# Bias products with a full contraction, a new order of the work between groups, and the second group's magnitude behind the first group's flags

## The chip, the cores and the metric

The kernel runs on 1 core of one Trainium2 chip. The metric is the device time in microseconds (us); lower is better. The engines are named as in the profile: PE is TensorE, DVE is VectorE, ACT is ScalarE, POOL is GpSimd, SP issues the transfers.

## The reference

A small transformer-like tower over 4 sequences of 512 tokens with 64 channels:

- token stage: for each sequence `weighted = where(mask, rel_dist, 0)`, `nbr = weighted @ neighbor_embed[ids] * w_rd`, then `h = [atom_embed[ids], nbr] @ w1 + b1`, a layer norm with gamma and beta, silu, `@ w2 + b2`.
- attention stage on the normalised h: `content`, `values` and `key_ph` are three projections of x with biases; `hop` and `ksk` are two-layer gelu networks that give query phases `tanh(...) * pi`, a width per head, and storage phases; cos and sin of these are features; the result is a causal (cumulative) sum over the sequence, which the kernel computes as scores against a triangle plus a running state, chunk by chunk. The five window weights `exp(-0.5 d^2 / width^2)` are folded into one phase (an arctangent of two sums) and one magnitude per head. A layer norm and an output projection follow.
- expert stage: 8 experts with 128 hidden units, the best two scores of each token chosen (`top 2`), `gelu(x @ W1 + b1) @ W2 + b2` summed over the chosen ones, with residuals to the output (4, 512, 64).

## The kernel before, in words

Four sequences make two groups (g = 0, 1) of two sequences each, side by side on the partitions. Each group has 8 tiles of 128 tokens (4 chunks times 2 sequences). For each group there are five stages, written as generators for each engine: `token` (T), `project` (P), `queries` (Q), `chunks` (C), `experts` (X), and `weights` (W) once. A generator gives up its turn at each `yield`. The list `ORDER` says in which order the pieces are issued, the same list on every engine: the third "P1" is the third piece of group 1's `project`. An engine runs its queue strictly in that order, and semaphores tie the engines to each other. So a piece that is moved in `ORDER` is moved past all that stands between, on every engine. In this text P1.3 means the third piece of P1.

The pieces that matter here:

- P1.1 (group 1): PE waits for the first query centres of group 0, runs ten filler products (`spin_products(n, bank)`, L624: n products of 128x512 bf16 into a bank that nobody reads), waits for x of group 1 and transposes it (L728). ACT copies the transposes to `x_t` (L447).
- P1.2: PE runs the position product (L761), then four "joint" products, one per chunk: a bias product (L735, stationary operand `ones[0:1, 0:P]`, one row, start of the accumulation) and the product with x_t (L737). Before, the order is joint 0, joint 1, `hop_and_gate` (L742, L745), joints 2 and 3. ACT copies each joint to `vk` (L453); joints 2 and 3 wait for the copies of 0 and 1, since they share two banks.
- P1.3: PE runs `storage` (L750, L752) and then fillers, each bunch behind a semaphore of group 0's query phases. ACT runs the gelus (L458 to L468).
- Q0.1 to Q0.8 and Q1.1 to Q1.8: window weights. Q.1: DVE L1303 to L1307, ACT exp (L489). Q.2: DVE phase base (L1314), ACT magnitude of the key phases (L495, Abs). Q.3: DVE window sums (L1320 to L1329), ACT key features by sine (L501). Q.4: DVE inverse root, the argument of the arctangent (L1340), then the query magnitude `mag` (L1342 to L1344); ACT, for group 1, eight multiplications of the stored keys (L509), then the arctangent (L512). Q.5: DVE phi and the phase sums (L1352 to L1362), ACT rounding (L518). Q.6: DVE L1368, ACT absolute value, sine, cosine. Q.7: DVE times `mag` (L1376). Q.8: DVE sums (L1383, L1387).
- C.1: PE transposes the key features into banks 4 and 5 (L843), ACT copies them (L542). C.2: the same for the queries (L860, L547). C.3: scores of chunk 0 (L871, L876). C.4 to C.7: per chunk the scores of the next one, the state product (L883, L885) and the outputs (L902 to L909); DVE masks the scores (L1401) and adds up the state (L1409, L1412). C.7: ACT squares and copies (L558, L559). C.8: PE variance and output projection (L927, L933), DVE inverse root (L1428 and behind). C.9: DVE `h3` (L1443), ACT its square.
- X.1: PE transposes h3 (L954). X.2: expert scores on PE (L963), the normalised x2 on DVE (L1466). X.3: low part of x2 on DVE (L1475), transposes on PE (L975), copies `xp1` on ACT (L583). X.4: DVE finds the two best experts and writes the flags (L1479 to L1497); PE, for group 0 only, runs 33 fillers behind semaphores. X.5: transposes with the flags (L995), copies `xp2` (L588). X.6 to X.24: n = 0 to 18, hidden products `hidden(n)` (L1014 with the high part of the weights, L1015 with the low part and the flags), gelu on ACT (L608), and second-layer products `back` (L1026, L1030). X.25: the results are turned back and added (L1041, L1049, L1507).

The group 0 experts (X0.6 on) run woven with the group 1 chunks (C1.2 on) in time on PE; after them the group 1 experts run alone.

Of the kernel before, what the change touches and what calls it, by code (L numbers as in the profile page):

```python
# [82 lines left out]
ORDER = ("T0 T0 T0 T0 T1 T1 T0 T0 T1 T0 T1 P0 P0 T1 P0 T1 Q0 P0 T1 W0 P0 Q0 P1 Q0 P1 Q0 C0 Q0 Q0 P1 Q0 Q0 P1 C0 "  # L83
         "C0 P1 C0 P1 C0 Q1 C0 Q1 C0 Q1 C0 C0 X0 X0 Q1 X0 C1 Q1 Q1 X0 Q1 X0 X0 X0 X0 Q1 X0 C1 C1 X0 C1 X0 C1 "
# [21 lines left out]
def tower(nc, ids, dist, mask, early, folded, late, ffn, mrows, out):  # L106
# [4 lines left out]
    with ExitStack() as ctx:  # L111
# [156 lines left out]
        hid_bank = (0, 1, 3)  # L268
        ksk_bank = (2, 6)
# [28 lines left out]
        def pair(t, c):  # L298
            return t[:, c, :, :].rearrange("p f d -> p (f d)")

# [103 lines left out]
        def _(act):  # L404
# [82 lines left out]
            def queries(g):  # L487
# [3 lines left out]
                act.wait_ge(S["kq_tanh"], g + 1)  # L491
                act.wait_ge(S["st_tanh"], g + 1)
                if g:
                    act.wait_ge(S["k_feat"], 2 * g)
                nc.scalar.activation(kph_abs[:], kph[:, g], ACT.Abs).then_inc(S["kph_abs_set"], 1)  # L495
                yield

                act.wait_ge(S["kph_abs_set"], g + 1)
# [6 lines left out]
                if g:  # L505
                    act.wait_ge(S["k_feat"], 2 * g + 1)
                    act.wait_ge(S["gcr_set"], 2)
                    for t in range(8):
                        ins = nc.scalar.mul(feat[:, g, 0, t, D:P], feat[:, g, 0, t, D:P], gcr[:, g, t:t + 1])  # L509
                    ins.then_inc(S["stored_q"], 1)  # L510
                act.wait_ge(S["at_arg"], g + 1)
                nc.scalar.activation(wscr[:, 3], wscr[:, 2], ACT.Arctan).then_inc(S["at_set"], 1)  # L512
# [60 lines left out]
            def experts(g):  # L573
# [7 lines left out]
                for k in range(2):  # L581
                    act.wait_ge(S["xp1_mm"], 2 * g + k + 1)
                    nc.scalar.copy(xp1[g][:, 512 * k:512 * k + 512], bank[x_bank[g] + k][:, :]).then_inc(S["xp1_set"], 1)  # L583
                yield
                yield
# [14 lines left out]
                for n in range(19):  # L600
                    if n == 10:
                        copy_y(0)
                    if n < 16:
# [4 lines left out]
                        nc.scalar.activation(hid[:, at % HB], bank[hid_bank[at % 3]][:, :], ACT.Gelu).then_inc(S["hid_set"], 1)  # L608
# [10 lines left out]
        def _(pe):  # L619
# [98 lines left out]
            def project(g):  # L718
                pe.wait_ge(late_in, 16)
                if g:  # L720
                    pe.wait_ge(S["center_set"], 1)
                    spin_products(10, 2)
# [10 lines left out]
                def joint(c, i):  # L733
                    if g:
                        nc.tensor.matmul(bank[i][:, 0:VK], ones[0:1, 0:P], K["vk_b"][0:1, :], start=True, stop=False)  # L735
# [30 lines left out]
                if g:  # L766
                    hop_and_gate()
                    last_joints()
                    yield
                    pe.wait_ge(S["h1_norm"], NG)  # L770
# [12 lines left out]
                    spin_products(4, 7)  # L783
# [46 lines left out]
            def chunks(g):  # L830
# [33 lines left out]
                def scores(c):  # L864
                    at = g * NC + c
                    pe.wait_ge(S["qtr_set"], 2 * g + c // 2 + 1)
                    pe.wait_ge(S["ktr_set"], 2 * g + 2)
                    if c:
# [74 lines left out]
            def experts(g):  # L943
# [33 lines left out]
                yield  # L977
                if g == 0:
# [634 lines left out]
```

## Time and profile before

| | |
|---|---|
| time, median of 3 runs | 165.93 us (165.22 to 165.97) |
| the profiled execution's own time | 166.21 us |
| its span, first to last instruction | 164.5 us (so 1.71 us lie around it) |
| PE busy | 151.8 us, 92% of the span, fillers included (L624: 120 recorded, 30.0 us) |
| DVE busy | 113.7 us, 69% |
| ACT busy | 83.6 us, 51% |
| mean granted TensorE clock | 0.976 of full speed |

PE looks full, but 30.0 us of it are fillers. Where fillers stand, PE is the bound only if they run past the event that the next real product waits for. So the share of busy time does not answer the question; in each stretch one looks for the event that comes last. The digits of the clock are tenths of full speed; 5 is the lower of the two levels.

### The profile page before, as it was taken

Reading aid. Unit: us, or ns where it says so; the run is one execution under the profiler, and the core shown is the slowest. Engines: PE = TensorE matmul, PEld = TensorE weight load, DVE = VectorE, ACT = ScalarE, POOL = GpSimd, SP = SyncE. Lnnn points to the kernel's source line nnn. Section 1 sums busy time; section 2 is a strip of 40 time slices with the busy share of each in tenths; the row PEclk is TensorE's granted clock in tenths of the full one; section 3 lists DMA queues with packets and bytes.
Section 4 is the critical chain, followed back from the end, with each engine's and each line's share of the span. In section 5 each row is a group of like instructions: output and inputs, shape, how many; then the busy total and the mean of one; then the engine's idle time right before and its main releaser. Section 6 shows DMA issues by size and latency. Waiting matters only on the chain.

```text
span 164.5 us, 2374 instructions
## 1 busy us (share of the span) xinstructions
PE 151.8 (92%) x810; PEld 85.7 (52%) x816; DVE 113.7 (69%) x339; ACT 83.6 (51%) x149; POOL 8.9 (5%) x38
## 2 busy tenths in 40 slices
PE   5899999989997999999998797999999999899991
PEld 1383465328773425447887345464675554563530
DVE  6999979977798982998679887894433798041202
ACT  3001151479298713994357548976314366645621
POOL 5301300140000000000000000000000000000000
PEclk9999999999999559999999999999999999999998
DMA  4999950300000000000000000000000000002011
GB/s 123 333 421 429 421 225 6 128 0 0 0 0 4 2 0 0 0 2 0 4 0 0 0 4 0 0 0 2 4 0 0 0 4 0 0 0 63 2 32 32
DMA packets 3779, 9.21 MB, mean 56 GB/s; under 512 B 2356, under 2 KB 2484, under 8 KB 3256
## 3 DMA queue, kind: packets, MB, share of 16 engines
q1 hardware_dynamic: 3768, 9.08, 14.8%
q8 instruction: 6, 0.10, 0.3%
q14 instruction: 5, 0.04, 0.1%
HBM read 8.55 MB, written 0.52 MB: 55 GB/s over the span
## 4 chain that ended last, share of the span: by engine, by line
PE 62%; DVE 28%; issue 5%; ACT 3%; POOL 0%; DVEq 0%; POOLq 0%
PE bank L1030 9%; PE bank L1014 6%; PE bank L624 5%; PE bank L1015 4%; PE bank L737 4%; PE bank L680 3%; DVE dist_sb L1155 2%; PE bank L658 2%; DVE invpos L1105 2%; PE bank L735 2%; PE bank L871 2%; PE bank L745 2%; PE bank L742 2%; DVE rs_v L1101 2%; PE bank L637 1%
## 5 line engine op out<-in xcount | busy, mean ns | idle before, releaser
L624 PE MATMUL bank<-spin 128*128 128x512 bf16 x120 | 30.0, 394 | 3.5 <-POOL spin L340 2.0
L608 ACT ACTIVATE hid<-bank 128x512 f32<-128x512 f32 x32 | 17.8, 602 | 19.3 <-PE bank L1015 19.3
L624 PEld LDWEIGHTS bank<-spin 128*128 128x128 bf16 x126 | 12.1, 101 | 18.3 <-issue 4.1
L1030 PE MATMUL bank<-hid,ffn_sb 128*64 128x512 f32 x64 | 16.4, 612 | 0.0
L1014 PE MATMUL bank<-xp,w1hi 128*128 128x512 f32 x32 | 14.6, 457 | 0.4 <-ACT xp L588 0.4
L1507 DVE TENSOR_TENSOR h<-bank,h 128x256 f32<-128x256 f32 (+1 forms) x5 | 1.8, 368 | 18.2 <-PE bank L1041 12.3
L1015 PE MATMUL bank<-xp,w1lo 128*128 128x512 f32 x32 | 12.6, 395 | 0.0
L1401 DVE TENSOR_TENSOR dist_sb<-bank,fold_sb 128x256 f32<-128x256 f32 x16 | 6.0, 419 | 7.9 <-PE bank L876 7.3
L1014 PEld LDWEIGHTS bank<-xp,w1hi 128*128 128x128 f32 x32 | 6.0, 188 | 7.5 <-ACT hid L608 3.8
L1155 DVE TENSOR_TENSOR dist_sb<-dist_sb,mask_in 128x1024 f32<-128x1024 f32 x8 | 9.2, 1218 | 0.0
L680 PE MATMUL bank<-dist_sb,neigh 128*64 128x512 f32 x32 | 9.0, 679 | 0.0
L409 ACT COPY neigh<-bank 128x512 f32<-128x512 f32 x2 | 1.2, 587 | 11.6 <-PE bank L658 11.6
L737 PE MATMUL bank<-fold_sb,proj 128*128 128x320 f32 x16 | 6.8, 534 | 0.0
L1030 PEld LDWEIGHTS bank<-hid,ffn_sb 128*64 128x64 f32 x64 | 3.4, 135 | 6.3 <-issue 3.6
L1015 PEld LDWEIGHTS bank<-xp,w1lo 128*128 128x128 f32 x32 | 6.1, 189 | 0.5
L680 PEld LDWEIGHTS bank<-dist_sb,neigh 128*64 128x64 f32 x32 | 3.0, 159 | 5.8 <-issue 4.8
L871 PE MATMUL bank<-dist_sb 64*128 64x256 f32 x16 | 5.6, 428 | 0.5 <-ACT dist_sb L547 0.5
L658 PEld LDWEIGHTS bank<-tables,onehot 100*128 100x128 f32 x32 | 5.4, 261 | 0.8 <-DVE tables L1126 0.8
L876 PE MATMUL bank<-dist_sb 64*128 64x128 f32 x32 | 5.7, 297 | 0.0
L658 PE MATMUL bank<-tables,onehot 100*128 100x64 f32 x32 | 5.6, 348 | 0.0
L1101 DVE TENSOR_REDUCE rs_v<-sq 128x8 f32<-128x520 f32 x6 | 4.1, 691 | 1.8 <-ACT sq L422 1.3
L453 ACT COPY vk<-bank 128x320 f32<-128x320 f32 x4 | 1.7, 420 | 7.0 <-PE bank L737 7.0
(275 smaller groups left out, 310.6 us busy)
## 6 DMA issues: line engine op xcount, KB each, us to landing
dist_sb<-in_dist SPq DMA_DIRECT2D x4, 1024.0 KB, 11.5
mask_in<-in_mask SPq DMA_DIRECT2D x2, 512.0 KB, 8.3
fold_sb<-in_folded SPq DMA_DIRECT2D x1, 998.0 KB, 11.3
ffn_sb<-in_ffn SPq DMA_DIRECT2D x1, 816.0 KB, 17.4
late_sb<-in_late SPq DMA_DIRECT2D x1, 728.5 KB, 16.0
mask_in<-in_mrows SPq DMA_DIRECT2D x1, 512.0 KB, 3.3
out<-h SPq DMA_DIRECT2D x8, 64.0 KB, 1.7
early_sb<-in_early SPq DMA_DIRECT2D x1, 167.0 KB, 2.3
```

The lines of the kernel that those rows point to most:

```text
L608: nc.scalar.activation(hid[:, at % HB], bank[hid_bank[at % 3]][:, :], ACT.Gelu).then_inc(S["hid_set"], 1)
L624: nc.tensor.matmul(bank[i][:, :], spin[:, 0:P], spin[:, :], start=True, stop=True)
L658: mm = nc.tensor.matmul(b3(5 if g == 0 else 7)[:, t], onehot[:, at:at + P], tables[:, D:2 * D], start=True, stop=True)
L680: mm = nc.tensor.matmul(rows(f), neigh[:, b, j], dist_sb[:, b, j], start=False, stop=(j == NC - 1), skip_group_check=True)
L737: nc.tensor.matmul(bank[i][:, 0:VK], x_t[:, c * P:(c + 1) * P], K["vk_bd"], start=(g == 0), stop=True).then_inc(S["vk_mm"], 1)
L871: nc.tensor.matmul(bank[4][:, 0:2 * P], k_t[lo, c, 0], q_t[lo, c].rearrange("p f i -> p (f i)"), start=True, stop=True).then_inc(S["s_mm"], 1)
L1014: nc.tensor.matmul(o, w1hi[:, e * HID:(e + 1) * HID], xp1[g][:, toks], start=True, stop=False)
L1015: nc.tensor.matmul(o, w1lo[:, e * HID:(e + 1) * HID], xp2[g][:, toks], start=False, stop=True).then_inc(S["hid_mm"], 1)
L1030: mm = nc.tensor.matmul(bank[2][j * D:(j + 1) * D, :], K["e_w2"][:, (e + j) * D:(e + j + 1) * D], hid[:, (at + j) % HB], start=False, stop ...
L1101: link(nc.vector.tensor_reduce(rs_v[:, 0:8], squares[:, :, :], AX_X, ALU.add))
L1155: nc.vector.tensor_tensor(dist_sb[:, b, rows], dist_sb[:, b, rows], mask_sb[:, b, rows], ALU.mult).then_inc(S["dist_masked"], 1)
L1401: nc.vector.tensor_tensor(s_m[:, c % 2, k], bank[4 + k][:, 0:2 * P].rearrange("p (f l) -> p f l", f=2), tri2, ALU.mult).then_inc(S["s_mask ...
```

## The change

What it does, edit by edit:

1. P1.1: 14 fillers instead of 10.
2. P1.2: the bias product has all 128 rows: the stationary operand is the first column of the identity, broadcast to 128 columns, the moving one all rows of `vk_b`. Joints 2 and 3 come before `hop_and_gate`, which goes to P1.3.
3. P1.3: the last four fillers go. In `ORDER` the piece C0.1 (key transposes and copies, group 0) moves from behind P1.2 to behind P1.3.
4. `ORDER`: Q1.1 moves from behind C0.5 to behind C0.2, Q1.2 from behind C0.6 to behind C0.4, C1.1 from behind X0.3 to behind X0.1. The Abs of group 1 moves from Q1.2 to Q1.3.
5. Q1.4: the arctangent comes behind two of the eight multiplications, the other six behind it. The three DVE instructions of `mag` for group 1 move to Q1.7.
6. X0.3/X0.4: ACT copies the second half of `xp1` in X0.4 (behind the sines). In X0.4 PE issues the high-part products of hidden tiles 0, 1 and 2 ahead, into banks 4, 5 and 3, between the fillers; three fillers go.
7. Group 0's experts: hidden products from n = 4 on are issued in pairs, (4, 5), (6, 7) and so on. The scores of group 1 wait for the gelus of hidden tiles 0 and 1 (banks 4 and 5).

```diff
-ORDER = ("T0 T0 T0 T0 T1 T1 T0 T0 T1 T0 T1 P0 P0 T1 P0 T1 Q0 P0 T1 W0 P0 Q0 P1 Q0 P1 Q0 C0 Q0 Q0 P1 Q0 Q0 P1 C0 "
-         "C0 P1 C0 P1 C0 Q1 C0 Q1 C0 Q1 C0 C0 X0 X0 Q1 X0 C1 Q1 Q1 X0 Q1 X0 X0 X0 X0 Q1 X0 C1 C1 X0 C1 X0 C1 "
+ORDER = ("T0 T0 T0 T0 T1 T1 T0 T0 T1 T0 T1 P0 P0 T1 P0 T1 Q0 P0 T1 W0 P0 Q0 P1 Q0 P1 Q0 Q0 Q0 P1 C0 Q0 Q0 P1 C0 "
+         "Q1 C0 P1 C0 Q1 P1 C0 C0 C0 Q1 C0 C0 X0 C1 X0 Q1 X0 Q1 Q1 X0 Q1 X0 X0 X0 X0 Q1 X0 C1 C1 X0 C1 X0 C1 "
...
+        first_bank = (4, 5, 3)
...
+        def hid_rows(at):
+            return bank[first_bank[at] if at < 3 else hid_bank[at % 3]][:, :]
...
-                act.wait_ge(S["kq_tanh"], g + 1)
-                act.wait_ge(S["st_tanh"], g + 1)
-                if g:
-                    act.wait_ge(S["k_feat"], 2 * g)
-                nc.scalar.activation(kph_abs[:], kph[:, g], ACT.Abs).then_inc(S["kph_abs_set"], 1)
-                yield
-
+                def magnitudes():
...
+                if g == 0:
+                    magnitudes()
+                yield
+
+                if g:
+                    magnitudes()
...
-                    for t in range(8):
+                    for t in range(2):
+                        nc.scalar.mul(feat[:, g, 0, t, D:P], feat[:, g, 0, t, D:P], gcr[:, g, t:t + 1])
+                act.wait_ge(S["at_arg"], g + 1)
+                nc.scalar.activation(wscr[:, 3], wscr[:, 2], ACT.Arctan).then_inc(S["at_set"], 1)
+                if g:
+                    for t in range(2, 8):
                         ins = nc.scalar.mul(feat[:, g, 0, t, D:P], feat[:, g, 0, t, D:P], gcr[:, g, t:t + 1])
                     ins.then_inc(S["stored_q"], 1)
-                act.wait_ge(S["at_arg"], g + 1)
-                nc.scalar.activation(wscr[:, 3], wscr[:, 2], ACT.Arctan).then_inc(S["at_set"], 1)
...
                     nc.scalar.copy(xp1[g][:, 512 * k:512 * k + 512], bank[x_bank[g] + k][:, :]).then_inc(S["xp1_set"], 1)
-                yield
-                yield
+                    if g == 0 and k == 0:
+                        yield
+                yield
+                if g:
+                    yield
...
-                    spin_products(10, 2)
+                    spin_products(14, 2)
...
-                        nc.tensor.matmul(bank[i][:, 0:VK], ones[0:1, 0:P], K["vk_b"][0:1, :], start=True, stop=False)
+                        nc.tensor.matmul(bank[i][:, 0:VK], ident[:, 0:1].broadcast_to([P, P]), K["vk_b"], start=True, stop=False)
...
                 if g:
+                    last_joints()
+                    yield
                     hop_and_gate()
-                    last_joints()
-                    yield
...
                     pe.wait_ge(S["cos_set"], 2)
-                    spin_products(4, 7)
...
                     pe.wait_ge(S["ktr_set"], 2 * g + 2)
+                    if g:
+                        pe.wait_ge(S["hid_set"], 2)
...
-                if g == 0:
-                    spin_products(3, 2)
+                def first_product(n):
+                    nc.tensor.matmul(hid_rows(n), w1hi[:, n * HID:(n + 1) * HID], xp1[0][:, 0:512], start=True, stop=False)
+
+                if g == 0:
+                    pe.wait_ge(S["w1_hi"], 2)
+                    pe.wait_ge(S["ktr_set"], 4)
                     pe.wait_ge(S["at_arg"], 2)
                     spin_products(6, 2)
+                    pe.wait_ge(S["xp1_set"], 1)
+                    first_product(0)
+                    first_product(1)
                     pe.wait_ge(S["phi_set"], 2)
...
+                    pe.wait_ge(S["score_read"], 1)
+                    first_product(2)
                     pe.wait_ge(S["first_best"], 1)
                     spin_products(7, 2)
...
-                    if n == E or (n == 1 and g == 0):
+                    if n == E or (n == 4 and g == 0):
...
-                    nc.tensor.matmul(o, w1hi[:, e * HID:(e + 1) * HID], xp1[g][:, toks], start=True, stop=False)
+                    if g or n >= 3:
+                        nc.tensor.matmul(o, w1hi[:, e * HID:(e + 1) * HID], xp1[g][:, toks], start=True, stop=False)
...
-                    if n < 16:
+                    if n < 16 and (g or n < 4):
                         hidden(n)
+                    elif n < 16 and n % 2 == 0:
+                        hidden(n)
+                        hidden(n + 1)
...
-                link(nc.vector.tensor_scalar(wden[:, :], wden[:, :], 1e-6, float(H * np.sqrt(PH)), ALU.add, ALU.mult))
-                link(nc.vector.reciprocal(wden[:, :], wden[:, :]))
-                nc.vector.tensor_tensor(mag[:, :], wscr[:, 0], wden[:, :], ALU.mult).then_inc(S["mag_set"], 1)
+                def magnitudes():
...
+                if g == 0:
+                    magnitudes()
...
                 yield
+                if g:
+                    magnitudes()
                 dve.wait_ge(S["mag_set"], g + 1)
```

## Rows read from the trace of the kernel before

**Rows 1.** The page's 40 slices of the span, the granted clock

```profile
PEclk9999999999999559999999999999999999999998
```

**Rows 2.** Half-microsecond windows: PE, PEld, DVE, ACT, POOL busy, clock, DMA share, GB/s

```profile
50.50:51.00 0.50, 0.00 (x0) 0.00 (x0) 0.50 (x1) 0.50 (x1) 0.00 (x0) 1.00 0.00 0
...
54.00:54.50 0.50, 0.50 (x3) 0.26 (x2) 0.50 (x1) 0.50 (x1) 0.00 (x0) 0.75 0.00 0
```

**Rows 3.** The chain of waits, 42 to 65 us: start, length, engine and line

```profile
42.60 1.08 PE bank L737 x4
...
53.49 0.54 PE bank L735 x2
...
55.15 1.36 PE bank L735 x2
...
62.81 0.73 PE bank L735 x2
...
64.32 0.43 ACT vk L453
```

**Rows 4.** DVE in order of time, 60 to 91 us: start, length, instruction, idle before

```profile
60.30 0.19 DVE L1340 TENSOR_TENSOR wscr<-csum,wscr 128x32 f32<-128x32 f32 x1
...
64.98 0.18 DVE L1354 TENSOR_SCALAR wscr<-wscr 128x32 f32<-128x32 f32 x1 [3.08 <-ACT wscr L512]
...
82.25 0.42 DVE L1295 TENSOR_TENSOR kph<-bank,late_sb 128x256 f32<-128x256 f32 x1 [0.92 <-PE bank L813]
...
84.59 0.17 DVE L1303 TENSOR_SCALAR wden<-tg 128x32 f32<-128x32 f32 x1
...
86.73 1.22 DVE L1314 TENSOR_TENSOR dist_sb<-dist_sb,half_turn 128x1024 f32<-128x1024 f32 x1
...
90.16 0.17 DVE L1428 TENSOR_SCALAR rs_q<-bank 128x8 f32<-128x8 f32 x1
```

**Rows 5.** ACT in order of time, 56 to 104 us

```profile
56.04 0.40 ACT L453 COPY vk<-bank 128x320 f32<-128x320 f32 x1
...
97.68 2.02 ACT L509 ACTIVATE feat<-feat,gcr 128x64 f32<-128x64 f32 x8
...
102.38 1.36 ACT L518 ACTIVATE thn<-dist_sb,even 128x512 f32<-128x512 f32 x2
```

**Rows 6.** PE in order of time, 86 to 115 us

```profile
86.96 0.44 PE L902 MATMUL bank<-dist_sb,vk 128*64 128x128 f32 x4 [0.54 <-DVE dist_sb L1412]
...
88.52 1.05 PE L927 MATMUL bank<-fold_sb,sq_c 128*128 128x2 f32 x8
...
101.57 7.29 PE L624 MATMUL bank<-spin 128*128 128x512 bf16 x32
...
113.62 1.09 PE L860 MATMUL bank<-fold_sb,feat 128*128 128x128 f32 x8
```

**Rows 7.** DVE in order of time, 98 to 113 us

```profile
98.32 0.17 DVE L1342 TENSOR_SCALAR wden<-wden 128x32 f32<-128x32 f32 x1
...
99.03 0.68 DVE L1475 TENSOR_TENSOR xhl<-hc,xhl 128x512 fp32r<-128x512 f32 x1
...
100.59 1.29 DVE L1362 TENSOR_TENSOR dist_sb<-dist_sb,phi 128x512 f32<-128x512 f32 x2
...
108.05 0.20 DVE L1497 TENSOR_SCALAR xhl<-xhl 128x64 fp32r<-128x64 f32 x1
...
112.56 0.49 DVE L1387 TENSOR_TENSOR feat<-q_sc 128x128 f32<-128x128 f32 x2
```

**Rows 8.** The chain of waits, 110 to 119 us

```profile
110.84 0.23 PE bank L1014
...
118.02 0.42 PE bank L1014
```

**Rows 9.** DVE and PE in order of time, 139 to 142 us

```profile
139.17 0.20 DVE L1497 TENSOR_SCALAR xhl<-xhl 128x64 fp32r<-128x64 f32 x1
...
140.49 1.09 PE L995 MATMUL bank<-fold_sb,xhl 128*128 128x128 f32 x8
```

More of the change, by code:

```diff
@@ L490, in queries @@
                 yield
-                act.wait_ge(S["kq_tanh"], g + 1)
-                act.wait_ge(S["st_tanh"], g + 1)
+                def magnitudes():
+                    act.wait_ge(S["kq_tanh"], g + 1)
+                    act.wait_ge(S["st_tanh"], g + 1)
+                    if g:
+                        act.wait_ge(S["k_feat"], 2 * g)
+                    nc.scalar.activation(kph_abs[:], kph[:, g], ACT.Abs).then_inc(S["kph_abs_set"], 1)
+                if g == 0:
+                    magnitudes()
+                yield
                 if g:
-                    act.wait_ge(S["k_feat"], 2 * g)
-                nc.scalar.activation(kph_abs[:], kph[:, g], ACT.Abs).then_inc(S["kph_abs_set"], 1)
-                yield
+                    magnitudes()
                 act.wait_ge(S["kph_abs_set"], g + 1)
@@ L607, in experts @@
                             act.wait_ge(S["y_mm"], (at - HB) // 2 + 1)
-                        nc.scalar.activation(hid[:, at % HB], bank[hid_bank[at % 3]][:, :], ACT.Gelu).then_inc(S["hid_set"], 1)
+                        nc.scalar.activation(hid[:, at % HB], hid_rows(at), ACT.Gelu).then_inc(S["hid_set"], 1)
                     if n == 18 and g == 0:
@@ L766, in project @@
                 if g:
-                    hop_and_gate()
                     last_joints()
                     yield
+                    hop_and_gate()
                     pe.wait_ge(S["h1_norm"], NG)
@@ L1011, in hidden @@
                         pe.wait_ge(S["hid_set"], 16 * g + n - 2)
-                    o = bank[hid_bank[(16 * g + n) % 3]][:, :]
+                    o = hid_rows(16 * g + n)
                     toks = slice(k * 512, (k + 1) * 512)
-                    nc.tensor.matmul(o, w1hi[:, e * HID:(e + 1) * HID], xp1[g][:, toks], start=True, stop=False)
+                    if g or n >= 3:
+                        nc.tensor.matmul(o, w1hi[:, e * HID:(e + 1) * HID], xp1[g][:, toks], start=True, stop=False)
                     nc.tensor.matmul(o, w1lo[:, e * HID:(e + 1) * HID], xp2[g][:, toks], start=False,
@@ L1340, in queries @@
                 nc.vector.tensor_tensor(wscr[:, 2], csum[:, 1], wscr[:, 1], ALU.mult).then_inc(S["at_arg"], 1)
-                link(nc.vector.tensor_scalar(wden[:, :], wden[:, :], 1e-6, float(H * np.sqrt(PH)), ALU.add, ALU.mult))
-                link(nc.vector.reciprocal(wden[:, :], wden[:, :]))
-                nc.vector.tensor_tensor(mag[:, :], wscr[:, 0], wden[:, :], ALU.mult).then_inc(S["mag_set"], 1)
+                def magnitudes():
+                    link(nc.vector.tensor_scalar(wden[:, :], wden[:, :], 1e-6, float(H * np.sqrt(PH)), ALU.add, ALU.mult))
+                    link(nc.vector.reciprocal(wden[:, :], wden[:, :]))
+                    nc.vector.tensor_tensor(mag[:, :], wscr[:, 0], wden[:, :], ALU.mult).then_inc(S["mag_set"], 1)
+                if g == 0:
+                    magnitudes()
                 if g == 0:
```

## The prediction

> **What bounds the kernel now.** I read the 40 slices first. The granted clock is full everywhere but in two slices, about 53 to 62 us [rows 1]. The half-microsecond windows place the fall at 54.25 us: 0.75 is the mean of half a window at full speed and half at the lower level (1.2 GHz) [rows 2]. Before it PE had stood still for some 0.9 us (the window at 50.5 shows 0.00 busy), and then ran, fillers and transposes apart, a product with 32 rows and the first bias product with one row. Next the chain of waits: in that stretch it is all PE, and it ends in the ACT copy of the fourth joint at 64.32 [rows 3]. Behind that copy in ACT's queue stands the arctangent of group 0, whose argument had been ready since 60.49 (60.30 + 0.19); DVE sat idle 3.08 us for it, until 64.98 [rows 4]. That is the largest single stall that the change touches. From there the chain is DVE (phases, masks, inverse roots), with PE filling; from 101.7 us it is PE with its own fillers [rows 6]; from 113.7 to 141 us PE is full with real products of experts and chunks; after 141 nothing is changed.
>
> **Step 1: joints, fillers and the clock (edits 1 to 3).** Four fillers more: ten take 2.1 us, so four take about 0.87 us and end near 51.2, where x arrives: cost nothing, and the empty 0.9 us before is covered. The bias product of one row takes 0.54 us at full speed, 1.36 at the lower level and 0.73 after the clock is back; a pair of joints with 128-row operands takes 1.08 for four instructions, 0.54 each half [rows 3]. So a joint costs 1.08 with all rows at full speed. Joints 0 and 1 run from 53.49 to 55.65. The copy of joint 0 can't begin before 56.04, when ACT has done its sines, and takes 0.40 [rows 5]; so joint 2 begins at 56.5, joint 3 ends at 58.65, its copy at 59.1. The argument of the arctangent is there at 60.49, which is now the last event. ACT gives the result at 60.75, but DVE itself goes on with mag and the stored keys until 61.9 and then reads it: L1354 at 61.95 in place of 64.98, **3.0 us earlier**. Next late is DVE itself. `hop_and_gate` and `storage`, moved behind, take 4.0 us on PE (to 62.7); ACT's gelus, which need them, start at 69.6, so nothing waits. The key transposes now wait behind the cosines of group 0 and fill the hole before the second-layer products; their copies (1.07 us) stand on ACT behind the gelus and before tg, where ACT idled 1.75 us. Nothing on this chain. Bounds: if the clock falls at 54.25 all the same, the four joints end at about 61.3 (two clean ones by 57.3, then the third by 59.4, the fourth across the rise), the copy at 61.8, and L1354 is at 62.1: 2.8 gained. If the pairs also keep the 0.2 to 0.3 us that each product lost in rows 3, the copy ends at 63.1 and 1.5 is gained. Upper end 3.1, the whole idle time. I take 3.0.
>
> By a rule of the Trainium skill (TensorE: Matmul & The Clock Gate, section HAM oscillation) the clock falls after long idle gaps of PE between bursts and holds while products are dense. By that rule full rows change nothing, for a one-row product is as busy as another; the page is silent on rows. The trace shows a fall though PE was idle for only 0.9 us in the stretch before it [rows 2]. With this rule the sum would hold 2.8 instead of 3.0.
>
> **Step 2: window weights moved up (edit 4).** Q1.1 takes DVE from 84.59 to 85.9, before the masking of the last chunk. The last outputs wait 0.54 us for DVE [rows 4, 6]. Moved to behind C0.2, Q1.1 (1.37 us) lies at 77.3 to 78.7 and holds up the first mask and the first centres by some 0.7 us; PE's centres run until 79.7 anyway, so the next scores don't notice, and the second centre and mask are 0.1 late. The phase base (1.22 us) goes into the idle 0.92 us before L1295 [rows 4] and makes that 0.3 late; PE is busy with the gate products by then and the next mask starts only at 83.7, so nothing follows. So the last outputs start about 0.45 us earlier (0.54 is the end), and the variance products, which end at 89.57, end at 89.1. DVE reaches L1428 at 90.16 because it was busy [rows 4, 6]; without the 2.6 us of Q1.1 and Q1.2 it is there at 88.5 and waits for them. **1.0 us** gained. Low end 0.3: if the masks slip by the 0.7 us that Q1.1 takes. High end 1.6: DVE's own time. The Abs of group 1 now lies behind the square on ACT; the sines then end at 91.9 (91.8 before), and h3 comes at 92.6 in this frame: hidden, with 0.7 to spare. C1.1 moved: 0.87 us of transposes and 1.07 of copies before the scores. On PE it pushes scores and fillers so that L975 comes at 99.3, on ACT it lies in an idle place.
>
> **Step 3: arctangent, magnitude, flags (edits 5, 6).** All in the frame of the old trace, from x2 on. The arctangent is behind two multiplications of 0.25 us (2.02 for eight [rows 5]) instead of eight: done at 98.7 in place of 99.8. The magnitude takes DVE from 98.32 to 99.03 [rows 7]; without it the phase sums start at 99.85 in place of 100.59, **0.7 earlier**. ACT: the six multiplications end at 100.1, half of xp1 at 100.6, and rounding starts at 100.65, in place of 102.38 where xp1 whole, and the key copies, stood before it [rows 5]: 1.7 earlier. With it L1368, the sines and the flags: L1497 ends at 106.5, not 108.25. PE: 33 fillers take 7.1 us and end after the flags, so PE's fillers are the bound of L995 there [rows 6]. Now there are 30 fillers (6.5) and three real products (0.23 each), without the key transposes (0.87): from 100.35 to 107.55, in place of 108.86: 1.3 earlier. PE is still the last one, by 1 us. xp2 and the first gelus follow 1.4 earlier; the high parts of tiles 0 to 2 are there, which saves another 0.2 before the first gelu. The query transposes of group 1 (113.69 in the chain, 113.62 with the modelled overlap [rows 6]) need two things: PE through back(0), at 111.95, and DVE's sums. The latter ended at 113.05 [rows 7], 4.9 us behind the flags; now 106.5 + 0.7 (mag) + 4.9 = 112.1. So they start at 112.15: **1.5 us earlier**. Low end 0.6: if the flags come only the 0.7 of the first sentence earlier, mag eats it and the sums end at 113.05 as before; the transposes then gain only the 0.6 by which they came behind the sums. High end 1.7 (PE alone). The new wait of the scores for two gelus (done at 110.5) is long over.
>
> **Step 4: pairs (edit 7).** A hidden product right behind another of its kind takes 0.23 us, one behind products of another shape 0.42 [rows 8]. Six pairs save six such changes, 1.2 us of PE between 115 and 140. But pairs put work earlier, so back-to-back waits for DVE appear: the variance products of C1.8 stand behind two hidden tiles and gain only 0.2; while h3 is awaited PE has 0.4 us less to do. From h3 on the flags of group 1 (139.37) are DVE's, and PE reaches L995 at 140.49 [rows 9]. PE can gain up to those 1.1 us plus 0.2; I get 139.8 by adding the pieces. **0.7 us**. Ends 0 and 1.3.
>
> **Sum.** 3.0 + 1.0 + 1.5 + 0.7 = 6.2. The profiled execution took 166.21 (span 164.5 and 1.71 around it): 160.0, span 158.3. The median of the runs shown lies 0.28 under the profiled one, so I forecast **159.7 us**. With the low ends of all four steps (1.5, 0.3, 0.6, 0) it would be 163.5, with the high ones (3.1, 1.6, 1.7, 1.3) 158.2.
>
> **Rivals.**
> - A, the full rows don't hold the clock: it falls near 54 us as before. For: the two-level fall came with only 0.9 us of idle time, and the 32-row product stays. Against: in P0 the same 32-row product follows an idle place too, and the slices there are at 9. The reordering of the joints saves most of it: 1.5 to 2.8 in place of 3.0, 160 to 161.2; I take 160.6.
> - B, a wait replaces steps 2 to 4: DVE's centres or ACT's queue (the exp table load now in the middle of the chunks, xp1's second half behind the sines) hold up PE. For: ACT has new work in front of the centres' tanh. Against: room of 0.7 us or more at each place I looked at. Steps 2 to 4 at their low ends: 3.0 + 0.9 = 3.9 gained, 162.0.
> - C, the clock falls elsewhere once, where PE now has holes (55.7 to 56.5, or 111.9). One stretch like that of rows 1 lasts 6.8 us and costs PE half of it, 3.4, where PE is the bound: 163.1.
> - D, slower than before: the pairing and the missing fillers let the clock fall at the start of the woven stretch (113 to 141), where the 64-row products of the chunks stand and nothing fills, and it stays down. Each microsecond at the lower level costs 0.5. Steps 1 to 3 and the pairs bring 6.2; so from 12.4 us at the lower level on the kernel is slower, and all 27 us cost 13.5 and give 173; with two stretches of 6.8 it is 166.5. For: such products are the least filled. Against: the same products run there now with 9 in every slice [rows 1], and pairs make PE denser, not thinner.
>
> **How the numbers follow.** The forecast 0.64 (own range 158.6 to 160.5), A 0.11, B 0.13, C 0.09, D 0.03. A change of 0.5% (0.8 us) is about what a measurement of this kernel can tell from none. All but D are beyond that on the fast side: faster 0.95, within 0.5% 0.02 (a mild D, or C and B together), slower 0.03. The range of 158.6 to 162.4 holds the forecast, A and B, and leaves out C, D and the far low end.
>
> **What would show it.** Step 1: the clock at 9 in all slices; L735 near 0.54 us; DVE's idle time before L1354 (the group 0 one) gone and that instruction at 62. Step 2: L1428 of group 0 waiting for PE L927, and at about 86.1. Step 3: the rounding of group 1 (L518) some 5.7 us earlier than now, PE's query transposes 5.5 earlier; L1497 of group 0 still ahead of PE's fillers. Step 4: L1014 at 0.23 for the second of each pair, and L995 of group 1 at 134.3. I am wrong if a slice of PEclk falls to 5 again, or if DVE's wait for ACT comes back before the phases.

## The result and the profile after

The changed kernel takes 160.2 us (median of 4 runs, 159.53 to 162.4), the kernel before 165.57 (4 runs, 163.83 to 165.97: the three shown ahead and one more). The ratio is 0.9682, 95% interval 0.9582 to 0.9782: 3.2% faster. The forecast was 159.7, range 158.6 to 162.4. The runs of both kernels spread by 2 to 3 us, with the mean clock that they were granted (told in the last section). A ratio leaves out only runs more than 1.5% above the shortest of the same kernel, so this one counts runs of the kernel before with a costly fall of the clock, and those of some experiments don't.

The changed kernel's profiled execution has a span of 159.0 us, 5.5 less than before, and took 160.67. First its page, the clock in 40 slices, which answers to [rows 1]:

```profile
PEclk9999999999999999999999999999999999999999
```

No 5 is left. Then DVE in order of time, which answers to [rows 4, 7] (L1370 was L1340, L1388 was L1354, L1325 was L1295, L1464 was L1428, L1511 was L1475, L1396 was L1362, L1533 was L1497, L1423 was L1387):

```profile
60.56 0.19 DVE L1370 TENSOR_TENSOR wscr<-csum,wscr 128x32 f32<-128x32 f32 x1
...
62.19 0.18 DVE L1388 TENSOR_SCALAR wscr<-wscr 128x32 f32<-128x32 f32 x1
...
79.66 0.42 DVE L1325 TENSOR_TENSOR kph<-bank,late_sb 128x256 f32<-128x256 f32 x1
...
86.63 0.17 DVE L1464 TENSOR_SCALAR rs_q<-bank 128x8 f32<-128x8 f32 x1 [0.88 <-PE bank L944]
...
94.79 0.68 DVE L1511 TENSOR_TENSOR xhl<-hc,xhl 128x512 fp32r<-128x512 f32 x1
...
96.27 1.30 DVE L1396 TENSOR_TENSOR dist_sb<-dist_sb,phi 128x512 f32<-128x512 f32 x2
...
102.65 0.20 DVE L1533 TENSOR_SCALAR xhl<-xhl 128x64 fp32r<-128x64 f32 x1
...
107.98 0.49 DVE L1423 TENSOR_TENSOR feat<-q_sc 128x128 f32<-128x128 f32 x2
```

The wait of 3.08 us behind the arctangent is gone: L1388 follows its neighbour without idle time. Before L1464 the order of need has turned round: DVE, which came last [rows 4], now idles 0.88 us for the variance products. PE in order of time answers to [rows 3, 6, 9]:

```profile
53.69 0.81 PE L751 MATMUL bank<-fold_sb 128*128 128x320 f32 x2
...
56.76 0.81 PE L751 MATMUL bank<-fold_sb 128*128 128x320 f32 x2 [0.65 <-ACT vk L457]
...
70.60 1.06 PE L802 MATMUL bank<-late_sb,proj 128*128 128x8 f32 x8 [0.52 <-ACT proj L462]
...
85.47 1.05 PE L944 MATMUL bank<-fold_sb,sq_c 128*128 128x2 f32 x8
...
103.69 1.04 PE L1021 MATMUL bank<-fold_sb,xhl 128*128 128x128 f32 x8
...
108.53 1.09 PE L875 MATMUL bank<-fold_sb,feat 128*128 128x128 f32 x8
...
126.27 0.50 PE L1053 MATMUL bank<-xp,eb 32*128 32x512 f32 x1 [0.48 <-ACT proj L614]
...
133.93 1.08 PE L1057 MATMUL bank<-hid,ffn_sb 128*64 128x512 f32 x4 [0.22 <-ACT hid L624]
...
134.94 1.09 PE L1021 MATMUL bank<-fold_sb,xhl 128*128 128x128 f32 x8
```

The reader sees the copy of joint 0 as the new wait before joint 2 (0.65 us, covered), and two new waits of PE for ACT near the end, 0.48 and 0.22 us; the trace without pairs (below) has neither. The chain of waits shows a pair, first and second tile, as in [rows 8]:

```profile
115.71 0.43 PE bank L1041
116.14 0.23 PE bank L1042
116.37 0.23 PE bank L1041
```

In the traces of the fourteen kernels x of group 1 begins between 49.5 and 51.1 us, although no edit touches what leads to it. Why is open, but for what the last section says of it. So from here on the executions are compared by the time since DVE begins x of group 1 (L1243 before, L1273 after). Each column is a start in the profiled execution minus that start; the last is the span's end:

```
                            phi(0)  root(0)  query transposes(1)  first hidden(1)  end
before                      14.93   39.67    63.13                91.53            114.01
changed                     11.87   35.87    57.77                85.71            108.24
before, 14 fillers          11.87   36.61    60.05                88.45            110.95
before, full rows           11.87   37.88    61.34                89.73            112.15
changed, one row            11.87   38.06    59.95                87.91            110.37
changed, hop first          11.87   35.86    57.75                85.70            108.14
changed, no pairs           11.87   35.87    57.77                86.18            108.62
changed, mag in front       11.87   35.87    58.30                86.23            108.65
changed, all muls first     11.88   35.88    58.56                86.50            108.91
changed, weights late       11.88   36.62    58.51                86.46            108.96
changed, fewer fillers      11.88   35.88    57.79                85.74            108.22
changed, ACT order          11.88   35.87    57.78                84.74            107.23
the same, flags first       11.88   35.87    57.77                84.83            107.35
combined                    11.89   35.88    57.19                84.25            106.72
```

phi(0) is the start of L1356 or L1390, root(0) of L1428 or L1464, the query transposes of L860 or L875, the first hidden product that of group 1. Where two lines differ by less than 0.03 us before an edit, they repeat each other: the columns resolve 0.1 us, which the times of whole runs don't.

### The profile page after: what moved, and what is told of

It reads as the page before. It is cut to its first block, busy times and chain, and to the rows that moved or that the text cites. A ratio compares the mean times of both kernels' runs of the same rounds, so it can differ in the third digit from the quotient of the medians.

```text
span 159.0 us, 2379 instructions
## 1 busy us (share of the span) xinstructions
PE 147.1 (93%) x813; PEld 85.6 (54%) x813; DVE 113.7 (72%) x339; ACT 83.2 (52%) x149; POOL 8.8 (6%) x38
## 4 chain that ended last, share of the span: by engine, by line
PE 48%; DVE 37%; issue 7%; ACT 6%; POOL 0%; DVEq 0%; POOLq 0%
PE bank L1057 8%; PE bank L1041 5%; PE bank L1042 4%; PE bank L696 3%; DVE q_sc L1412 2%; DVE dist_sb L1185 2%; PE bank L674 2%; PE bank L888 2%; DVE invpos L1135 2%; DVE q_sc L1419 2%; DVE rs_v L1131 2%; DVE dist_sb L1402 2%; PE bank L753 1%; PE bank L816 1%; PE bank L919 1%
## 5 line engine op out<-in xcount | busy, mean ns | idle before, releaser
L640 PE MATMUL bank<-spin 128*128 128x512 bf16 x123 | 31.1, 394 | 2.7 <-POOL spin L344 2.0
L624 ACT ACTIVATE hid<-bank 128x512 f32<-128x512 f32 x32 | 17.3, 601 | 15.3 <-PE bank L1042 15.2
L640 PEld LDWEIGHTS bank<-spin 128*128 128x128 bf16 x123 | 11.5, 101 | 18.1 <-issue 4.4
L1057 PE MATMUL bank<-hid,ffn_sb 128*64 128x512 f32 x64 | 16.5, 610 | 0.2 <-ACT hid L624 0.2
L1041 PE MATMUL bank<-xp,w1hi 128*128 128x512 f32 x29 | 12.8, 440 | 0.7 <-ACT xp L604 0.4
L1041 PEld LDWEIGHTS bank<-xp,w1hi 128*128 128x128 f32 x29 | 5.4, 187 | 7.6 <-issue 4.2
L1057 PEld LDWEIGHTS bank<-hid,ffn_sb 128*64 128x64 f32 x64 | 3.6, 135 | 5.2 <-ACT hid L624 3.1
L753 PE MATMUL bank<-fold_sb,proj 128*128 128x320 f32 x16 | 5.4, 438 | 0.0
L1412 DVE TENSOR_TENSOR q_sc<-q_sc,mag 128x512 f32<-128x512 f32 x8 | 5.0, 688 | 0.0
```

What stands on the lines that cost most here:

```text
L624: nc.scalar.activation(hid[:, at % HB], hid_rows(at), ACT.Gelu).then_inc(S["hid_set"], 1)
L640: nc.tensor.matmul(bank[i][:, :], spin[:, 0:P], spin[:, :], start=True, stop=True)
L753: nc.tensor.matmul(bank[i][:, 0:VK], x_t[:, c * P:(c + 1) * P], K["vk_bd"], start=(g == 0), stop=True).then_inc(S["vk_mm"], 1)
L1041: nc.tensor.matmul(o, w1hi[:, e * HID:(e + 1) * HID], xp1[g][:, toks], start=True, stop=False)
L1057: mm = nc.tensor.matmul(bank[2][j * D:(j + 1) * D, :], K["e_w2"][:, (e + j) * D:(e + j + 1) * D], hid[:, (at + j) % HB], start=False, stop ...
L1412: nc.vector.tensor_tensor(q3, q3, bc(mag[:, 16 * k:16 * k + 16], PH), ALU.mult).then_inc(S[done], 1)
```

## Experiments on step 1: what held the clock

**One row again.**

```diff
-nc.tensor.matmul(bank[i][:, 0:VK], ident[:, 0:1].broadcast_to([P, P]), K["vk_b"], start=True, stop=False)
+nc.tensor.matmul(bank[i][:, 0:VK], ones[0:1, 0:P], K["vk_b"][0:1, :], start=True, stop=False)
```

> The changed kernel, but the bias products of group 1 again with one row (stationary operand ones[0:1, 0:P]); the 14 fillers and the late hop_and_gate stay. Theory 1 (the rows hold the clock, the new order brings the time): the clock falls again near 54 us, or, where it doesn't, each bias product and its partner take 0.73 us in place of 0.54; either way the fourth copy is over by 61.9 us and DVE's phase chain (L1388) starts at most 1.2 us later than 62.2; time within 1.3 us of the changed kernel. Theory 2 (the rows alone bring the 2.8 us): phase chain near 65 us, time some 2.8 us up. Rival (the clock falls only for the idle place that the fillers cover): no fall of the clock, and no change but 0.2 us per product.

Measured: 162.87 us (162.51 to 163.2, 4 runs). The half-microsecond windows (columns as in [rows 2]) show the fall, here at 57.5 and not at 54, and PE in order of time what comes of it:

```profile
57.00:57.50 0.50, 0.50 (x2) 0.30 (x2) 0.43 (x4) 0.00 (x0) 0.00 (x0) 0.99 0.00 0
57.50:58.00 0.50, 0.50 (x2) 0.00 (x0) 0.43 (x3) 0.00 (x0) 0.00 (x0) 0.50 0.00 0
64.00:64.50 0.50, 0.50 (x2) 0.02 (x1) 0.43 (x1) 0.50 (x1) 0.00 (x0) 0.68 0.00 0
```

```profile
54.63 0.80 PE L751 MATMUL bank<-fold_sb,ones 1*128 1x320 f32 x2
...
59.60 1.44 PE L753 MATMUL bank<-fold_sb,proj 128*128 128x320 f32 x2
...
66.30 5.56 PE L640 MATMUL bank<-spin 128*128 128x512 bf16 x24
71.69 1.04 PE L858 MATMUL bank<-fold_sb,feat 128*128 128x128 f32 x8
72.57 0.96 PE L802 MATMUL bank<-late_sb,proj 128*128 128x8 f32 x8
```

The other three runs are as long as the traced one, 162.6 to 163.2. DVE's phi is not a tenth later, within what theory 1 said. But the time is 2.1 to 2.2 us up, where theory 1 had at most 1.3: PE comes out of the slow stretch late, still has 24 fillers to run before the key transposes, and begins the second-layer products at 72.57 in place of 70.60 (2.3 us later, counted from x), and in the columns it is 2.2 us late from there on. The fall costs 2.1 here and 3.06 in the kernel before, by another path. In this order of work the full rows are needed; which part of the new order makes it so was not tried.

**hop_and_gate first again** (full rows and fillers kept).

```diff
-                    last_joints()
-                    yield
                     hop_and_gate()
+                    last_joints()
+                    yield
```

> The changed kernel, but hop_and_gate again between joints 1 and 2 (full rows and 14 fillers stay). Theory 1: with the clock up, joints 2 and 3 come 2.0 us of hop_and_gate later less the 0.7 us in which PE now idles: fourth copy at 60.5 in place of 59.65, just about the time of the arctangent's argument (60.75), so DVE's phase chain stays at 62.2 and the time is the same within 0.3 us. Theory 2 (the order is what brings the gain): phase chain 1 to 3 us later and the time with it.

Measured: 160.38 us (160.16 to 160.88), all columns as the changed kernel. Theory 1 holds: with the clock up, the new order of the joints brings nothing.

**Full rows alone, in the kernel before.** The same edit of L735.

> The kernel before with the full-row bias products alone. Theory 1 (rows hold the clock): no slice near 54 to 61 us at 5, hop_and_gate in 2.0 us in place of 3.5, fourth copy near 60.5 and the 3.08 us wait of DVE for the arctangent gone or under 0.5; 2.5 to 3 us faster than before (162.8). Rival A (the clock falls for the idle place before, or the 32-row product): the clock falls all the same, PE's pairs 1.07 each; fourth copy near 62.7, 1.4 us faster.

Measured: 164.99 us (162.22 to 165.82). phi(0) is 3.06 us earlier, as with a clock that holds, and the fourth copy is in time, though PE again stood still for 0.92 us before x (first line). So the full rows, too, are enough against the fall at 54. But the clock falls later:

```profile
51.79 0.60 PE L624 MATMUL bank<-spin 128*128 128x512 bf16 x2 [0.92 <-DVE x L1243]
...
70.89 1.06 PE L787 MATMUL bank<-late_sb,proj 128*128 128x8 f32 x8 [0.96 <-ACT proj L458]
...
74.01 1.92 PE L860 MATMUL bank<-fold_sb,feat 128*128 128x128 f32 x8
```

```profile
71.50:72.00 0.50, 0.50 (x6) 0.48 (x6) 0.47 (x3) 0.48 (x1) 0.00 (x0) 1.00 0.00 0
72.00:72.50 0.50, 0.50 (x6) 0.50 (x6) 0.47 (x2) 0.00 (x0) 0.00 (x0) 0.94 0.00 0
74.00:74.50 0.50, 0.50 (x4) 0.49 (x3) 0.47 (x2) 0.00 (x0) 0.00 (x0) 0.50 0.00 0
```

At 72.4 (0.94 is the mean of 0.44 us at full speed and 0.06 at the lower level), after 0.96 us of idle time and products of 8 and 2 columns, where the old order has nothing to fill: the transposes take 1.92 us in place of 1.04, and root(0) comes 1.3 later than with 14 fillers. Neither theory had that. In the changed kernel the key transposes stand in that place, its idle time is 0.52 (L802 above) and the clock stays. But it also stands still for 0.68 us just before those transposes, and this trace for 0.30 before its last fillers: 1.20 us in all against 1.26. So the length of the idle time hardly parts the two, and why one falls is not shown. Nor is this fall the full rows' alone: the traced run and one other have a mean clock of 0.990 (165.0), and so have one of fourteen runs of the kernel before (165.1) and one of ten with 14 fillers (165.1). The other two runs here are 162.22 at 0.979 and 165.82 at 0.976, and the last looks like the kernel before with its fall at 54 us; it has no trace.

**14 fillers alone, in the kernel before.**

```diff
-                    spin_products(10, 2)
+                    spin_products(14, 2)
```

> The kernel before with 14 fillers in place of 10 alone. Theory 1 (rows): the clock falls as before, time as before. Rival (the 0.9 us of idle time before x is what lets it fall): no fall, the DVE wait before the phases shrinks from 3.08 to about 0.5 us, time 2.5 us less.

Measured: 163.39 us (162.32 to 165.12, 10 runs), against 165.16 for the kernel before beside it (162.43 to 166.3, 14 runs). The clock in 40 slices, and DVE:

```profile
PEclk9999999999999999999999999999999999999998
```

```profile
61.68 0.18 DVE L1354 TENSOR_SCALAR wscr<-wscr 128x32 f32<-128x32 f32 x1
```

The rival is right: with one-row products and the old order, but without the 0.9 us of idle time, the clock doesn't fall in this trace before the last microseconds, the DVE wait is gone, and phi(0) is 3.06 us earlier. Nine of its ten runs are below 163.8, but only six of the fourteen beside them. The ratio, which counts only six of those fourteen, is 0.9999 (0.9962 to 1.0035): against runs without the costly fall the fillers are worth nothing, and holding the clock is all that they do. So in the old order four fillers alone bring step 1.

## Experiments on steps 2 to 4

**Window weights late**: Q1.1 and Q1.2 back behind C0.5 and C0.6.

```diff
-"Q1 C0 P1 C0 Q1 P1 C0 C0 C0 Q1 C0 C0 X0 C1 ..."
+"C0 P1 C0 P1 C0 Q1 C0 Q1 C0 Q1 C0 C0 X0 C1 ..."
```

> The changed kernel with Q1.1 and Q1.2 back behind C0.5 and C0.6. Theory (DVE's 2.6 us lie in idle places in the changed kernel): last outputs of group 0 0.3 us later, DVE is the last one before the inverse root again, which comes 0.8 us later; time 0.8 us up. Rival (the root was bound by the variance products anyway): 0.3 us or less.

Measured: 161.42 us (160.26 to 162.95); root(0) 0.75 later, and that is carried to the end (0.72). DVE in order of time:

```profile
83.07 0.75 DVE L1437 TENSOR_TENSOR dist_sb<-bank,fold_sb 128x256 f32<-128x256 f32 x2
...
87.16 0.16 DVE L1359 TENSOR_SCALAR rs_q<-gsum 128x8 f32<-128x8 f32 x1
87.36 0.17 DVE L1464 TENSOR_SCALAR rs_q<-bank 128x8 f32<-128x8 f32 x1
```

No idle time before L1464: DVE is last again. The theory (0.8 later) holds.

**All multiplications first**: eight in the loop before the arctangent, none behind.

```diff
-                    for t in range(2):
+                    for t in range(8):
...
-                if g:
-                    for t in range(2, 8):
```

> The changed kernel with all eight multiplications before group 1's arctangent. Theory (the arctangent's place is what brings step 3): arctangent at 96.3 in place of 94.9, DVE waits some 0.9 us for it, rounding, flags and sums 0.9 us later, time 0.9 us up. Rival (ACT's rounding is bound by ACT's own queue, whose sum is the same): under 0.3 us.

Measured: 160.76 us (160.17 to 161.88); query transposes 0.79 later, end 0.67. DVE waits for ACT again, 0.82 us where the theory had 0.9:

```profile
94.43 0.17 DVE L1383 TENSOR_SCALAR wscr<-csum 128x32 f32<-128x32 f32 x1
95.42 0.18 DVE L1385 TENSOR_SCALAR wscr<-wscr 128x32 f32<-128x32 f32 x1 [0.82 <-ACT wscr L522]
```

**The magnitude in front**: the three instructions back in Q1.4.

```diff
-                if g == 0:
-                    magnitudes()
+                magnitudes()
...
-                if g:
-                    magnitudes()
```

> The changed kernel with group 1's magnitude back in Q1.4, ahead of group 0's flags. Theory (DVE's sums of group 1 bound the query transposes, and the magnitude only changes its place within the same DVE chain): phases 0.7 us later, flags 0.6 later, sums of Q1.8 within 0.15 us of the changed kernel, time the same. Rival (the flags bound, through PE and xp2): everything behind is 0.6 to 0.7 us later.

Measured: 160.6 us (160.1 to 161.49). The sums of Q1.8 come 0.12 earlier, as expected, but the query transposes 0.53 later. The theory is wrong, and the rival has the size right. PE:

```profile
95.23 1.09 PE L992 MATMUL bank<-fold_sb,xhl 128*128 128x128 f32 x8 [0.45 <-DVE xhl L1508]
...
103.35 1.04 PE L1021 MATMUL bank<-fold_sb,xhl 128*128 128x128 f32 x8
...
107.04 1.08 PE L1057 MATMUL bank<-hid,ffn_sb 128*64 128x512 f32 x4
108.05 1.09 PE L875 MATMUL bank<-fold_sb,feat 128*128 128x128 f32 x8
```

PE has no idle time at 108.05: x2's low part (xhl) stood behind the magnitude on DVE and comes 0.7 later, so L992 waits 0.45 us for it, and PE's 30 fillers pass that on. The flags are 0.7 later too (done at 102.54), but L1021 starts 0.81 behind them without idle time. So it is xhl that passes the delay on, not the flags.

**Fewer fillers**: 3 in place of 7 after the first best score.

```diff
-                    spin_products(7, 2)
+                    spin_products(3, 2)
```

> The changed kernel with 3 fillers in place of 7 after the first choice of experts (group 0). Theory (PE's own fillers and DVE's sums end within 0.1 us of each other before group 1's query transposes, so neither alone gives anything): the transposes with the flags 0.8 us earlier, the first gelu 0.3 us earlier (ACT's table load then bounds), query transposes within 0.1 us, first hidden product of group 1 and time unchanged. Rival (the fillers alone are the bound, as a reading of the run with the magnitude in front would have it): 0.4 us or more gained at the query transposes.

Measured: 160.39 us (159.59 to 162.46), columns unchanged within 0.03. PE:

```profile
101.84 1.09 PE L1021 MATMUL bank<-fold_sb,xhl 128*128 128x128 f32 x8
...
107.47 1.09 PE L875 MATMUL bank<-fold_sb,feat 128*128 128x128 f32 x8 [0.72 <-DVE feat L1423]
```

The flags' transposes are 0.8 us earlier, counted from x, and PE gives it all back in a wait of 0.72 us for DVE's sums. In the changed kernel L875 starts 1.16 us behind the start of L1057, 1.01 with the magnitude in front, where only PE's queue holds it. So the two bounds of the query transposes, PE's queue and DVE's sums, lie within 0.2 us of each other; undoing an edit of one side loses, and easing one side alone gains nothing.

**No pairs**: `if n < 16 and (g or n < 4)` becomes `if n < 16`.

> The changed kernel with the hidden products of group 0 issued one by one again from n = 4. Theory (PE-bound stretch, each pair saves the 0.2 us of a change of shape, waits for ACT give part of it back): from the query transposes of group 1 to the first hidden product of group 1, 27.9 us in the changed kernel, becomes 28.4 to 28.5; time up by 0.5. Rival 1 (the saving is full): 1.2 us up. Rival 2 (the waits eat it all): no change.

Measured: 160.53 us (159.83 to 162.68). From the query transposes to the first hidden product of group 1: 28.41 in place of 27.94, so 0.47. The theory is right; the saving is not the full 1.2. (The whole times, 160.53 against 160.2, don't resolve this.)

**ACT order**: where those 0.7 us went. In the changed kernel ACT's copy of y (L614) stands behind a square that waits for DVE:

```profile
125.11 0.63 ACT L576 ACTIVATE sq<-h 128x512 f32<-128x512 f32 x1 [2.98 <-DVE h L1479]
125.65 0.57 ACT L614 COPY proj<-bank 128x512 f32<-128x512 f32 x1
```

The edit takes that copy ahead of the square, and gelu 15 ahead of the copies of xp1:

```diff
-                    if n == 10:
+                    if g and n == 10:
                         copy_y(0)
...
+                    tiles = () if n > 15 or (g == 0 and n == 15) else (14, 15) if g == 0 and n == 14 else (n,)
...
+                    if n == 9 and g == 0:
+                        copy_y(0)
```

> The changed kernel with ACT's copy of y (first half, group 0) one piece earlier, ahead of the square of h3, and gelu 15 ahead of the xp1 copies of group 1. Theory (these two waits, 0.48 and 0.22 us of PE idle time, are what step 4 gave back): from the query transposes of group 1 to its first hidden product 27.2 to 27.3 us in place of 27.9; 0.7 us faster. Rival (the flags of DVE bound the last stretch): no more than 0.2.

Measured: 159.3 us (158.49 to 161.26); that stretch 26.96 in place of 27.94, 1.0 less, where the theory had 0.7. The two waits for ACT are shown as the cause: with them gone the back products run as one block, and the gain lies in these two places. From the transposes of h3 to the product behind them PE takes 0.58 us from start to start in place of 1.14, and for the last two groups of back products 1.87 in place of 2.31.

```profile
131.60 1.94 PE L1060 MATMUL bank<-hid,ffn_sb 128*64 128x512 f32 x8
133.47 1.09 PE L1024 MATMUL bank<-fold_sb,xhl 128*128 128x128 f32 x8
135.01 0.47 PE L1044 MATMUL bank<-xp,w1hi 128*128 128x512 f32 x1 [0.44 <-ACT xp L604]
```

**Flags first**: the same, and X1.5 before X0.23 in `ORDER`.

> e10 and, in ORDER, the transposes with group 1's flags and their copies (X1.5) ahead of group 0's last back products, so that the xp2 copies lie beside PE. Theory: the 1.5 us from the end of those back products to the first hidden product shrink to about 0.9 of transposes; 1.5 us less than the changed kernel in all. Rival (the copies of y, now behind, bound the hidden products): as e10.

Measured: 159.45 us (158.56 to 161.55); nothing gained over the last run (27.06). The rival's outcome, by another cause: PE now stands 0.40 us waiting for DVE's flags, and the back products, 1.0, lie behind them:

```profile
132.34 1.09 PE L1024 MATMUL bank<-fold_sb,xhl 128*128 128x128 f32 x8 [0.40 <-DVE xhl L1536]
133.37 1.08 PE L1060 MATMUL bank<-hid,ffn_sb 128*64 128x512 f32 x4
134.38 0.50 PE L1044 MATMUL bank<-xp,w1hi 128*128 128x512 f32 x1
```

**Combined**: that, with 3 fillers and two of the three magnitude instructions at the end of Q1.3, in DVE's idle 0.88 us.

```diff
+                if g:
+                    link(nc.vector.tensor_scalar(wden[:, :], wden[:, :], 1e-6, float(H * np.sqrt(PH)), ALU.add, ALU.mult))
+                    link(nc.vector.reciprocal(wden[:, :], wden[:, :]))
...
```

> e11, with 3 fillers in place of 7 as in e9, and the first two of group 1's three magnitude instructions in the place where DVE idles 0.88 us before the inverse root. Theory: both bounds of the query transposes move, by 0.6 (DVE) and 0.4 (PE, behind ACT's table load): 0.4 us less than e11, 1.9 less than the changed kernel, 158.3 in a run without a fall of the clock. Rival (fewer fillers let the clock fall behind them): a fall near 105 to 112 us and up to 3 us lost.

Measured: **158.22 us** (158.04 to 159.44, 6 runs), ratio to the kernel before 0.9602 (0.954 to 0.9665); counted from x of group 1 it is 1.52 us shorter than the changed kernel (1.9 expected). The query transposes gain the 0.58 that DVE's shorter chain gives, and no fall of the clock came of the missing fillers in its trace. It is the fastest version tried. Five of its six runs have a mean clock of 0.973 to 0.976 and its trace has the fall in the token stage that goes with shorter runs (last section); the sixth, at 0.999, took 159.44, 1.2 less than the changed kernel at 1.0.

## Why the prediction was right

The total: 5.5 us less span, forecast 6.2. The start of the trace is 0.27 us later than before, which no step speaks of; the steps make 5.77.

- **Step 1, 3.0 forecast, 3.06 measured** (14.93 to 11.87). The working held piece by piece: L751 and L753 take 0.54 each between starts, joint 3 ends at 59.0, the arctangent's argument is last. That the clock would hold was right; the prediction did not part the fillers from the rows. In the old order either is enough against the fall at 54 us, the fillers (nine of ten runs without a costly fall) or the rows (the clock holds there in that trace). With rows alone two of four runs are longer at a clock of 0.990; in the traced one of them the fall is at 72.4 us. In the new order the rows are needed beside the fillers (four runs). The fallback of rival A, that the new order saves most of the gain when the clock falls, is refuted by the run with one row: 2.1 us lost in place of 0.2 to 1.5. The step that failed there is "`hop_and_gate` and `storage`, moved behind, ... so nothing waits": it was worked out at the full clock only. The sentence that used the Trainium skill (TensorE: Matmul & The Clock Gate, HAM oscillation) named idle gaps as the cause of a fall, not rows. The run with 14 fillers speaks for it, in that removing 0.9 us of idle time is enough. Two runs speak against its being all: with one row PE stood still for only 0.26 us between x and the fall, and with full rows alone the clock held at 54 us behind 0.92 us of idle time, where by that sentence full rows would have changed nothing.
- **Step 2, 1.0 forecast, 0.74 measured** (root: 36.61 in the run with 14 fillers, 35.87 now; the run with the weights late gives 0.75). The turn of the bound from DVE to the variance products came as said. Mis-sized was the gain of the last outputs: 0.45 forecast, 0.28 measured (L902 started 33.41 after x, step 1 taken off: 86.96 - 50.49 - 3.06; L919 now starts 33.13 after it: 83.89 - 50.76). The rest is small: L1464 starts 0.11 behind the end of the variance products (85.47 + 1.05).
- **Step 3, 1.5 forecast, 1.54 measured** (60.05 to 57.77 less 0.74). Both bounds came out about where the working had them, less than 0.2 us apart (it took 4.9 us from the flags to the sums, where its rows give 113.05 - 108.25 = 4.8). The two undoing runs lose 0.8 for the arctangent's place and 0.5 for the magnitude's; with two bounds so near each other such losses need not add up to the gain. The high parts ahead took the place of fillers and were not tried alone.
- **Step 4, 0.7 forecast, 0.46 measured.** The cause, waits for ACT, is another than the prediction named (waits for DVE, "back-to-back waits for DVE appear"): gelu 15 stands behind the xp1 copies in ACT's queue, and the first copy of y behind a square that waits for DVE. The run with ACT's order mended gives 1.0 more. So it was right that waits would take back a part of the 1.2, and wrong which.
- **Against the median.** 159.7 forecast, 160.2 measured, and part of that closeness is luck. The profiled execution, at a clock of 1.0, took 160.67, where the working had 160.0 (0.4 of the difference is in the steps, 0.27 is the later start). Two of the other runs, 159.53 and 159.74, have a mean clock of 0.978; the traced run with fewer fillers has the same clock and 159.59, and its fall lies in the token stage, where it goes with runs some 1 us shorter (last section). Without these two the median would lie higher. The fourth run is at 162.4 with 0.989. The kernel before has its costly fall in a part of its runs only: in three further sets of 14, 7 and 11 runs its median was 165.16, 163.77 and 165.38. So what the median gains depends on how often a fall comes: with no fall on either side the gain is about 2.8 us (before at clock 0.997: 163.4 to 163.8; changed at 1.0: 160.67), which is steps 2 to 4.
- Rival C, one fall elsewhere, at 163.1, is what the run at 162.4 looks like, though there is no trace of that run. It is no single case: the runs without pairs, with the weights late and with fewer fillers each have one at a clock of 0.989, 162.5 to 163.0. B came only in the two small waits for ACT of step 4, and D didn't come.

## To carry to other kernels

Fillers, products with full rows and a new order may cure the same fall of the clock: try each alone, and price a fall with all that stands behind it on PE, fillers too. Where two bounds have been made equal, undoing an edit shows a loss and extending it shows nothing, so read which engine stands idle. When products are paired on one engine, their readers in the other engine's queue have to be moved as well.

## What the runs showed of the hardware

- The mean clock of the same kernel differs from run to run, so its falls do; where they lie is known for the one traced run of each kernel. Of 14 runs of the kernel before on one chip, those with a mean clock of 0.997 took 163.4 to 163.5, one with 0.979 took 162.4, those with 0.976 took 166.0 to 166.3 (the trace above is such a one, with its fall at 54 us), one with 0.990 took 165.1, and those with 0.953 to 0.958 took 165.2 to 165.6. Between the runs at 0.997 and those at 0.976 lie 2.7 us.
- A fall is not always a loss. In seven of the fourteen traces the clock is at the lower level from about 8 to 15 us, in the token stage; in six of these x of group 1 starts at 49.5 to 49.8, earlier than in any trace without that fall (50.3 to 51.1); in the seventh (ACT order) it starts at 50.3. With the magnitude in front, two runs with a mean clock of 0.978 took 160.1 and two with 1.0 took 161.1 and 161.5. The changed kernel shows the same: 159.5 and 159.7 at 0.978, 160.7 at 1.0. Why a run with this fall is shorter stays open.
- A bias product of one row between products of 128 rows takes 0.73 us from start to start at the full clock (54.63 to 55.36 in the run with one row), and so does its full-row partner where a one-row product follows (53.90 to 54.63). The bias product with all rows takes 0.54 (54.87 to 55.41 in the changed kernel), although it does 128 times the multiplications.
